# Cross-attention and a routed expert layer on one core: moving the entry of the attention loop, and building the rows of the first four expert tiles with 0/1 matrices

## The reference, cut to what matters

```python
x = x + xattn(layernorm(x), ctx, ctx, mask, Wq, bq, Wk, bk, Wv, bv, Wo, bo)
x = x + moe(layernorm(x), gate_w, w1, b1, w2, b2)
```

## Time and profile before

| | us |
|---|---|
| median of three executions | 330.65 |
| the profiled execution, its own time | 331.22 |
| its span (first to last instruction) | 329.5 |

### The profile page before, as it was taken

How to read it: one execution, slowest core, us unless ns; L and a number is a source line. 1 busy time by engine, 2 the same in 40 slices (tenths; PEclk the granted TensorE clock), 3 DMA queues, 4 the chain that set the end, 5 groups by cost and what they waited for, 6 DMA issues and landing times.

```text
span 329.5 us, 6252 instructions
## 1 busy us (share of the span) xinstructions
PE 258.2 (78%) x1856; PEld 125.8 (38%) x1856; DVE 172.0 (52%) x422; ACT 231.5 (70%) x365; POOL 78.6 (24%) x134
## 2 busy tenths in 40 slices
PE   2689858599999998989999999985474079999940
PEld 2455535212212121212222222234463079898940
DVE  4798952235453535354535454448751327676622
ACT  4348674489999999999999999961794025555520
POOL 8892002000100100000101000402057604444430
PEclk9999995789999999999999999999898569999995
DMA  7999680010101010101001010199301171101114
GB/s 201 371 400 402 204 172 2 17 29 2 40 0 39 12 28 12 28 12 27 21 19 26 14 32 8 40 374 270 54 33 49 49 186 34 33 26 33 34 35 187
DMA packets 28931, 29.29 MB, mean 89 GB/s; under 512 B 15262, under 2 KB 22834, under 8 KB 28785
## 3 DMA queue, kind: packets, MB, share of 16 engines
q1 hardware_dynamic: 27456, 26.21, 26.3%
q0 software_dynamic: 1456, 2.86, 2.8%
HBM read 21.62 MB, written 7.45 MB: 88 GB/s over the span
## 4 chain that ended last, share of the span: by engine, by line
issue 29%; PE 25%; ACT 16%; DVE 12%; POOL 5%; SPq 5%; DMA 4%; DVEq 2%; ACTq 1%; POOLq 0%
ACT w2T L996 8%; ACT arenaB L996 8%; PE bank L1282 7%; PE bank L1401 5%; PE bank L1264 5%; SPq L318 4%; PE bank L1409 3%; POOL qS L380 2%; DVE arenaC L528 2%; DVE arenaB L899 2%; SPq L290 1%; PE bank L1170 1%; DMA x_sb<-in_x_dram 1%; DMA arenaA<-ys_dram 1%; DVE arenaB L905 1%
## 5 line engine op out<-in xcount | busy, mean ns | idle before, releaser
L716 DVE TENSOR_TENSOR arenaA<-bank,arenaA 128x512 f32<-128x512 f32 x80 | 55.2, 690 | 81.7 <-PE bank L1282 81.7
L996 ACT ACTIVATE arenaB<-bank 128x1024 f32<-128x1024 f32 x80 | 77.5, 1022 | 7.6 <-PE bank L1264 5.6
L996 ACT ACTIVATE w2T<-bank 128x1024 f32<-128x1024 f32 x80 | 76.7, 1028 | 2.9 <-PE bank L1264 1.6
L1264 PE MATMUL bank<-qS,keys 64*128 64x512 bf16 x324 | 63.7, 395 | 13.0 <-ACT w2T L996 5.7
L1264 PEld LDWEIGHTS bank<-qS,keys 64*128 64x128 bf16 x324 | 15.3, 93 | 101.3 <-ACT w2T L996 50.1
L1026 ACT ACTIVATE mask_u<-bank,arenaB 128x128 f32<-128x128 f32 x92 | 26.3, 369 | 39.2 <-PE bank L1401 39.2
L1282 PE MATMUL bank<-arenaB,vcur 128*32 128x512 f32 x320 | 44.3, 627 | 1.1
L1282 PE MATMUL bank<-w2T,vcur 128*32 128x512 f32 x320 | 42.6, 605 | 0.0
L402 POOL CAST keep<-flags 128x1 f32 x11 | 2.1, 189 | 143.7 <-DVE arenaC L628 143.0
L472 POOL DMA_INDIRECT ys_dram<-arenaB,mask_u x23 | 22.3, 969 | 34.9 <-DVE arenaB L905 34.9
L1401 PE MATMUL bank<-arenaB 128*128 128x128 f32 x184 | 27.2, 295 | 2.3 <-DVE arenaB L891 2.3
(11 more groups left out here) (300 smaller groups left out, 319.1 us busy)
## 6 DMA issues: line engine op xcount, KB each, us to landing
mask_u<-in_L_ffn_w_dram SPq DMA_DIRECT2D x2, 2048.0 KB, 10.4
mask_u<-in_mask_BxSxS_bk_dram SPq DMA_DIRECT2D x6, 560.5 KB, 12.5
ctx_sb<-in_ctx_dram SPq DMA_DIRECT2D x3, 768.0 KB, 13.2
qS<-qparts_dram SPq DMA_DIRECT2D x4, 448.0 KB
mask_u<-in_mask_BxSxS_bk_dram SPq DMA_DIRECT2D x6, 240.0 KB, 11.3
keys_in<-kparts_dram SPq DMA_DIRECT2D x40, 32.0 KB
mask_u<-in_mask_BxSxS_bk_dram SPq DMA_DIRECT2D x1, 1121.0 KB, 7.6
xs_dram<-w1T SPq DMA_DIRECT2D x2, 520.0 KB, 17.1
```

The lines of the kernel that those rows point to most:

```text
L716: nc.vector.tensor_tensor(a, bank[:, 4 + k % 2, :], a, ALU.add).then_inc(s["ac"], 1)
L996: nc.scalar.activation(probs[u % 8], bank[:, 2 * (u % 2):2 * (u % 2) + 2, :].rearrange("p a b -> p (a b)"), ACT.Exp, scale=SCALE).then_inc ...
L1264: last = mm(bank[:, 2 * (u % 2) + a, :], keys[rows, g, :], qS[rows, g, cols], start=not hides, stop=True, tile_position=(64 * a, 0))
```

## The change

The loop's edge: units 2 and 3 of the first tile are issued ahead of the loop, with `hide` as for units 0 and 1, and `tile_steps` becomes values k, unit 2k+4, unit 2k+5. ACT passes two increments of `ex` at the end, for two units that nobody reads. The zeroing of `arenaA` goes from ACT to POOL, `mask_turn(0)` ahead of `first_keys`, DVE's copy of the mask ahead of `shift_col`, POOL's first `tile_in` ahead of the clearing of `fill`. `keep_busy` issues products that nobody reads at three places (7, 4 and 12).

The first four expert tiles: DVE builds, for tile j, a 0/1 matrix of tokens by places (`places`), and PE multiplies the tokens in SBUF with it (`tile_rows`, eight products), in place of the scatter, the load and the turn. These tiles run before the loads of `xs_sb` are waited for; their results are kept (`y_first`) and weighted later, when the weights have come with the second load. The part of b2 is multiplied behind tile 1 and added behind tile 3. All 16 scatters stay. `xs_dram` is filled by seven DMAs (before: three), and loaded by five.

```diff
+FIRST = 4
+SPARE = [[j] for j in range(FIRST)] + [list(range(FIRST + b, NT, 3)) for b in range(3)]
+XS_CUTS = [(FIRST, 6), (0, FIRST), (6, 12), (12, 18), (18, NT)]
...
-            for b in range(3):
-                sp.dma_start(xs_dram.rearrange("(j s) c -> s j c", s=P)[:, b:NT:3, :],
-                             fill[:, b:b + 1, :].broadcast_to([P, len(range(b, NT, 3)), ROW])).then_inc(s["xs_fill"], 16)
+            for b, tiles in enumerate(SPARE):
+                sp.dma_start(xs_dram.rearrange("(j s) c -> s j c", s=P)[:, tiles[0]:tiles[-1] + 1:3, :],
+                             fill[:, b:b + 1, :].broadcast_to([P, len(tiles), ROW])).then_inc(s["xs_fill"], 16)
...
+            pool.wait_ge(s["qw"], 16 * len(Q_RUNS))
+            pool.wait_ge(s["qn_ps"], 1)
+            nc.gpsimd.memset(arenaA[:, :], 0.0).then_inc(s["ac"], 1)
             pool.wait_ge(s["plan_ready"], 1)
...
+            tile_in(plan[0:1, 1:2], s["cb"], s["kv"], 1, True)
             nc.gpsimd.memset(fill[:, :, :], 0.0).then_inc(s["fill"], 1)
...
-            with pool.Fori(1, n + 2) as i:
+            with pool.Fori(2, n + 2) as i:
...
-            for j in range(NT):
-                pool.wait_ge(s["yacc"], j + 2)
+            for j in range(FIRST):
+                pool.wait_ge(s["y_gated"], j + 1)
+                nc.gpsimd.indirect_dma_start(ys_dram, ..., y_first[:, j, :], None).then_inc(s["scat"], 16)
+            for j in range(FIRST, NT):
+                pool.wait_ge(s["yacc"], j + 1)
...
+            dve.wait_ge(s["mt"], 2)
+            nc.vector.tensor_copy(maskT[:, 0, :], maskT_ps).then_inc(s["mc"], 1)
             dve.wait_ge(s["bd_row"], 1)
             dve.wait_ge(s["rowkey"], len(COMBOS) + 4)
             nc.vector.tensor_tensor(shift_col[:, :], bank[:, 3, 64:65], shift_rows[:, :], ALU.mult).then_inc(s["bias"], 1)
-            dve.wait_ge(s["mt"], 2)
-            nc.vector.tensor_copy(maskT[:, 0, :], maskT_ps).then_inc(s["mc"], 1)
...
+            nc.vector.tensor_tensor(at_tile, both, offset..., ALU.subtract).then_inc(s["own"], 1)
+            nc.vector.tensor_scalar(below_end, at_tile, P - 0.5, None, ALU.is_lt).then_inc(s["own"], 1)
+            nc.vector.scalar_tensor_tensor(at_tile, at_tile, 1.0, below_end, ALU.add, ALU.mult).then_inc(s["own"], 1)
+            nc.vector.tensor_tensor(own, at_tile[:, :, 0:QT], at_tile[:, :, QT:2 * QT], ALU.max).then_inc(s["own"], 1)
+            def places(j):
+                if j >= 3:
+                    dve.wait_ge(s["T_ps"], j - 2)
+                nc.vector.tensor_tensor(token_place[j % 3], own[:, j, :]....broadcast_to([P, QT, P]),
+                                        ramp....broadcast_to([P, QT, P]), ALU.is_equal).then_inc(s["own"], 1)
+            for j in range(3):
+                places(j)
             for k in range(2):
                 dve.wait_ge(s["gT_ps"], k + 1)
...
             stage(0)
+            slot_rows(0)
             stage(1)
-            slot_rows(0)
             slot_rows(1)
-            for j in range(NT):
+            for j in range(3, FIRST):
+                places(j)
+            for j in range(FIRST):
+                if j + 2 < FIRST:
+                    stage(j + 2)
+                    slot_rows(j + 2)
+                dve.wait_ge(s["yps"], j + 1)
+                nc.vector.tensor_copy(y_first[:, j, :], bank[:, 4 + j % 2, 0:P]).then_inc(s["yacc"], 1)
+            dve.wait_ge(s["b2ps"], 1)
+            nc.vector.tensor_tensor(x2, x2, bank[:, 6:8, :]..., ALU.add).then_inc(s["b2ps"], 1)
+            stage(FIRST)
+            stage(FIRST + 1)
+            slot_rows(FIRST)
+            slot_rows(FIRST + 1)
+            dve.wait_ge(xs_in[1], 16)
+            dve.wait_ge(s["yacc"], FIRST)
+            for j in range(FIRST):
+                nc.vector.tensor_scalar(y_first[:, j, :], y_first[:, j, :], xs_sb[:, j, D:D + 1], None, ALU.mult).then_inc(s["y_gated"], 1)
+            for j in range(FIRST, NT):
...
-            nc.scalar.activation(arenaA..., ones..., ACT.Copy, scale=0.0).then_inc(s["ac"], 1)
...
+            act.wait_ge(s["pv"], n * 8 + 4)
+            act.sem_inc(s["ex"], 2)
             nc.scalar.preload_act_table(ACT.Sqrt)
...
+            def keep_busy(to, times):
+                for _ in range(times):
+                    mm(to, identb[:, :], pick[:, 0:512], start=True, stop=True)
...
                 if c == 12:
+                    keep_busy(bank[:, 2, :], 7)
                     key_sums(1)
...
+            keep_busy(bank[:, 7, :], 4)
             project(0, s["cb"], s["kv"], True)
...
+            mask_turn(0)
             pe.wait_ge(s["kch"], 4)
             first_keys(0, 4)
...
             project(1, s["cb"], s["kv"], True)
+            scores(0, 2, 2, 0, True)
+            scores(0, 3, 3, 0, True)
             pe.wait_ge(s["cs_sb"], 2)
...
                 for k in range(8):
-                    scores(i, (2 * k + 2) % 16, 2 * k + 2, i + (k == 7), hides)
-                    scores(i, (2 * k + 3) % 16, 2 * k + 3, i + (k == 7), hides)
-                    values(i, k)
+                    values(i, k)
+                    scores(i, (2 * k + 4) % 16, 2 * k + 4, i + (k >= 6), hides)
+                    scores(i, (2 * k + 5) % 16, 2 * k + 5, i + (k >= 6), hides)
...
                 last.then_inc(s["at_ps"], 1)
+            keep_busy(b6, 12)
             pe.wait_ge(s["x2s"], 4)
...
-            pe.wait_ge(s["slot"], 8)
-            pe.wait_ge(s["b2_in"], 32)
+            pe.wait_ge(s["wtb_sb"], 2 * E)
...
-            pe.wait_ge(s["yacc"], 1)
-            pe.wait_ge(s["wtb_sb"], 2 * E)
...
+            def tile_rows(j):
+                pe.wait_ge(s["ln2"], QT)
+                pe.wait_ge(s["own"], j + 5)
+                if j >= 2:
+                    pe.wait_ge(s["T_sb"], j - 1)
+                for t in range(QT):
+                    last = mm(bank[:, j % 2, 0:P], xn2[:, t, :], token_place[j % 3][:, t, :], start=(t == 0), stop=(t == QT - 1))
+                last.then_inc(s["T_ps"], 1)
...
-            slots_turn(0)
-            slots_turn(1)
+            tile_rows(0)
+            tile_rows(1)
             up(0)
-            for j in range(NT):
+            for j in range(FIRST):
+                if j + 1 < FIRST:
+                    up(j + 1)
+                if j + 2 < FIRST:
+                    tile_rows(j + 2)
+                down(j)
+                if j == 1:
+                    b2_products()
+            slots_turn(FIRST)
+            slots_turn(FIRST + 1)
+            up(FIRST)
+            for j in range(FIRST, NT):
```

More of the change, by code:

```diff
@@ L1306, in tile_steps @@
                 for k in range(8):
-                    if k == 7:
+                    values(i, k)
+                    if k == 3 and hides:
+                        mask_turn(i + 1)
+                    if k == 6:
                         pe.wait_ge(s["kc"], i + 4)
@@ L1411, in down, with b2_products @@
                 last.then_inc(s["yps"], 1)
-            slots_turn(0)
-            slots_turn(1)
-            up(0)
-            for j in range(NT):
+            def tile_rows(j):
[6 more added lines that the diff above has]
+                last.then_inc(s["T_ps"], 1)
+            def b2_products():
+                pe.wait_ge(s["b2_in"], 32)
+                pe.wait_ge(s["gT_sb"], 2)
+                for t in range(QT):
+                    last = mm(bank[:, 6 + t // 4, (t % 4) * P:(t % 4 + 1) * P], epi_e[:, t * P:(t + 1) * P], b2_sb[:, :], start=True, stop=True)
+                last.then_inc(s["b2ps"], 1)
+            pe.wait_ge(s["slot"], 5)
+            tile_rows(0)
+            tile_rows(1)
+            up(0)
+            for j in range(FIRST):
[10 more added lines that the diff above has]
+            for j in range(FIRST, NT):
                 if j + 1 < NT:
```

78 lines of the change are left out of this document (46 added, 32 removed).

## The result

Median of the kernel after: 324.88 us (324.33 to 325.38, 4 executions), beside 330.68 us (330.41 to 331.18) for the kernel before: ratio 0.9827, 95% interval 0.9801 to 0.9853. The profiled execution took 324.56 us, its span 322.8 us, against 331.22 us: 6.66 us gained by the two profiled executions, 5.8 by the medians, forecast 5.0. The sign and nearly the size are right. The parts are not. The table shows when each mark of the program is reached, in us from the start of the span.

What follows compares the result with a forecast made beforehand. ACT was taken to bound the loop, and POOL's scatters, then PE, the expert layer. Gains of 2.8 - 0.1 + 2.3 = 5.0 us off 331.22 gave 326.2, as a median 325.7 us; range 323.4 to 330.1.

Steps and rivals of the forecast that it cites:

- First exponential: Ahead of the attention loop: first exponential at 55.7 us in place of 57.35, gain 1.65, bounds 0.75 and 2.75.
- the price of the zeroing: Clearing arenaA on POOL ahead of the loop: takes 4 us, at most about 14.5, and costs the path 0.
- Entering the loop: Loop's start: entry stall covered by two exponentials, exponential 4 at 64.2 us; gain taken 2.8, bounds 1.3 and 4.3.
- The steady loop: Attention loop's later tiles: nothing changes, since ACT is the bound and PE's order between two edges is the same.
- the third rival: Loop's edge comes to light: 10 tiles lose 0.87 us each, 3.7 slower in all, 334.4 us; chance 5%.
- Up to the weights: From the loop's end to the expert weights: 12 fillers save 0.6 us (bounds 0 and 1.46), weights ready at 248.7.
- The first tiles: First four expert tiles, made without waiting for the scatters: gain 2.3 us, 0.6 of it from the weights.
- The joint: Between down(3) and up(4): DVE copies, adds b2, stages two tiles and copies turned rows; PE idle 3.5 us.
- The signs of being wrong: ACT idle in every tile, a gap around the b2 products, tile 4's turn awaiting its load, row products at 4 us.
- The clock: Rival: TensorE's clock stays down despite the fillers, only 1.8 us gained, 328.8 us; chance 12%.
- The b2 products: Rival: these products end late between tiles 1 and 2, costing 4.4 of the 5.0 us, 330.1 us; chance 15%.
- The scatters: Rival: under a busier DVE they run over 7.2 us late and use up the slack, 327 to 329 us; chance 5%.

Runs made afterwards that it cites:

- Run 5: The kernel after with the zeroing of arenaA back on ACT: ratio 0.9864 to the kernel before.
- run 10: The kernel after with the 11 early filler products (7 and 4) narrowed to one column: ratio 1.0025 to the kernel before.
- run 6: The kernel after with the zeroing on ACT and without the 7 and 4 early fillers: 337.12 to 340.48 us in five of six executions, 328.21 in one.
- run 7: The kernel after without the 12 fillers ahead of the ranks: ratio 1.0165 to the kernel before.
- run 8: The kernel after with zeroing on ACT, the loop turning between units 2 and 3, and the joint reordered: ratio 0.9779, from two of six executions.
- run 9: The kernel after, unchanged, timed again on run 10's chip: 335.5 to 337.2 us in five of six executions, 329.67 in one.
- run 12: The same kernel as run 8, timed once more: ratio 0.9802 to the kernel before, 324.02 to 325.95 us in four of six executions.
- run 11: The kernel before with 11 products of one column at the places of the early fillers: 326.94 us, ratio 0.9858.

## Why the prediction was right or wrong

**First exponential, 57.35 to 55.7: wrong**, at 57.53. The step that failed is the price of the zeroing: "I take 4, near ACT's own price, cost 0". Its length was right (3.51 us); what it runs beside was not asked. I had quoted the very rule, for the scatters only. Run 5, without that one edit, has 54.94: better than my 55.7 and inside the bound that I gave for a full clock (a gain of 2.75). The four fillers ahead of the projection, "0 taken", held it at half clock: it started at 49.86 us, 1.1 behind the start of DVE's copy of the context (48.75), where 0.3 was usual before and 0.3 is found with the narrow ones of run 10.

**Entering the loop: inside its bounds in size, wrong in mechanism.** I took 2.8 us (bounds 1.3 and 4.3), and exponential 4 came 3.99 us earlier. "The first values start 4.0 us behind exponential 1" failed: it was 61.02 - 59.47 = 1.55 us. The stall was not covered but gone, with the eleven fillers ahead of it; that they, meant for the clock, would do this was not foreseen. So exponential 4 came at 62.53, not 64.2: 1.8 late from the zeroing, 2.45 less stall, 1.0 from full clock. In run 6, where the stall stayed, ACT stood idle 4.97 us behind exponential 3, near the "3 to 4.5" foretold.

**The steady loop, "nothing changes": wrong by 0.16 us a tile**, 1.4 us in nine tiles. That is the third rival at a fifth of its price of 0.87. The end, for which I took 0.1 us, cost 0.01: the last exponentials come 2.89 us earlier and the turn of the sums 2.88.

**Up to the weights: 0.6 foretold, 0.92 found**, 1.4 by run 7. Not foreseen was the half clock at 225 to 232 us: products of 1.77 and 2.19 us in place of 1.20, 1.43 us on the path. Other executions of the same code (runs 8 and 10) do not have it.

**The first tiles: mis-sized.** 1.7 us foretold behind the weights (2.3 less 0.6), 4.43 found. From the first row product to the end of down(3): 17.24 us in place of 19.4, since eight row products cost their spacing, 1.79 us, and four products of up or down 0.9, not the length of their records, which I had taken for it (2.1 and 1.07). The joint took 3.19 for 3.5, with the clock low for 3.4 us behind it, as reckoned.

**The sum: nearly right, in part by luck.** Up to the weights 2.8 - 0.1 + 0.6 = 3.3 us were foretold and 2.37 found, in the first tiles 1.7 and 4.43. The price of the zeroing, the edge of the loop and the half clock at the gate took away what the vanished stall and the cheaper products gave.

**The signs of being wrong.** Two of the four came: ACT has an idle time in every tile, and the turn of tile 4 waits for its load, 0.40 us by the row at 265.58. The second costs nothing, since DVE copies the turned rows only at 268.03.

**The rivals.** The clock did not stay down in the tiles. (My reading of rows 6 was too strong: the 29 products of the slow stretch are 16 small bf16 products of the ranks, until 236.6 us, and then 13 turns. It rose with nothing but turns in the 2.6 us before.) The b2 products were not late in this execution; the effect is real and met other products, in runs 5 to 10 and 12. Its price of 4.4 us was too low, by the 5 to 12 us above, and its chance of 15% too low for other chips. The scatters lost 1.7 us, inside the slack, which was 2.2 us and not 7.2 (turned rows ready at 265.8, copied at 268.03). Beside a matrix of 1.22 us one scatter lost 0.35 us and one 1.0, more than my 0.2; beside DVE's copies, of which the rule that I quoted speaks, none of these took over 1.17 us, so there the trace again shows 0.2 and not a copy's full length of 0.43.

## What to carry to other kernels

Before anything moves to an idle engine, look at what runs beside it at that moment: a long write of POOL holds a copy or cast of DVE to its end. When an engine shows microseconds of issue behind a taken branch, try a dozen cheap instructions ahead of it before the order of the work is changed: of the 5.8 us that this change won, 4.7 were to be had so. An edge of a loop belongs where the engine waits anyway.

## What was not expected of the hardware

- One and the same taken branch lasts 0.4 us or 3.5 to 3.9 us, by whether eleven more products stand ahead of it (above).
- A memset of POOL holds a cast of DVE for 1.6 to 1.9 us and a copy of 0.23 us for 2.5 us.
- Products of float32 are signalled 3 to 7 us behind the ends of their records, on two of three chips in most executions of the kernels with row products, on the third in none of the four traces, two of them with row products; run 11 and the kernel before, without row products, have one such place each, where the scatters hide it. The Trainium skill, "Perfetto Trace Analysis", section "Tensor Engine Instruction (MATMUL, LD_WEIGHTS)", says that a product's end is estimated, not observed; that explains why the records don't show it, not why it happens. That is open, and so is the combination that these runs suggest, run 11 with the first tiles' part: it wasn't tried.
